# A third quarter buffer, evenly spaced conversions and 128-row stack reads in a fused attention and expert kernel on one core

## The reference, cut to what matters

```python
x = x + tanh(g_xattn) * attention(layernorm(x), ctx)      # x, ctx: 8 x 256 x 512, fp32
x = x + tanh(g_ffn) * experts(layernorm(x))               # 2048 tokens, 512 wide

def attention(x, c, Wq, bq, Wk, bk, Wv, bv, Wo, bo):      # over 256 channels, 16 heads of 16
    q, k, v = Wq @ x + bq, Wk @ c + bk, Wv @ c + bv       # per batch item, 256 x 512
    scores = einsum('bhkt,bhks->bhts', q, k) * 16 ** -0.5
    return Wo @ einsum('bhts,bhks->bhkt', softmax(scores), v) + bo

def experts(x):                                           # 12 experts, the 2 best for a token
    for e in range(12):
        h = silu(x @ w1[e].T) * (x @ w3[e].T)             # 320 hidden columns
        out += (h @ w2[e].T) * weight_of(e)               # softmax of the gate's 2 largest
```

## Time and profile before

| | us |
|---|---|
| median of 3 runs | 824.47 |
| the profiled execution, its span | 824.88, 823.1 |
| PE busy (x4217) | 646.0 |
| DVE busy (x757) | 415.7 |
| ACT busy (x391) | 316.8 |
| POOL busy (x186) | 243.8 |
| mean granted clock of PE | 0.888 |

### The profile page before, as it was taken

One profiled execution on the slowest core, in us unless ns is written; L12 is line 12 of the kernel. 1 busy time (PEld: TensorE's weight loads), 2 busy tenths in 40 slices (PEclk: granted clock), 3 DMA queues, 4 the chain that ended last, 5 costly groups with the idle time before them and its releaser, 6 DMA issues.

```text
span 823.1 us, 13989 instructions
## 1 busy us (share of the span) xinstructions
PE 646.0 (78%) x4217; PEld 282.8 (34%) x4218; DVE 415.7 (50%) x757; ACT 316.8 (38%) x391; POOL 243.8 (30%) x186
## 2 busy tenths in 40 slices
PE   4478897887885977978878654259999999999993
PEld 1112122212221222221221121236666666666661
DVE  5526476566584683774654843563333333333330
ACT  0047655554663554654646510002222222222221
POOL 5223123132240340331210202043344443354422
PEclk9999999889897997997987955559999999999997
DMA  6548669569579587695797636543677787754432
GB/s 205 129 104 204 209 212 293 146 191 310 156 217 293 146 227 262 192 251 159 238 251 211 203 106 230 174 156 63 174 188 195 213 242 201 204 105 92 85 51 39
DMA packets 66405, 150.82 MB, mean 183 GB/s; under 512 B 9973, under 2 KB 15606, under 8 KB 64822
## 3 DMA queue, kind: packets, MB, share of 16 engines
q1 hardware_dynamic: 34576, 72.37, 31.5%
q10 hardware_dynamic: 22150, 55.35, 20.3%
q0 software_dynamic: 9632, 22.55, 14.1%
HBM read 87.85 MB, written 57.93 MB: 177 GB/s over the span
## 4 chain that ended last, share of the span: by engine, by line
PE 50%; DVE 16%; DMA 15%; issue 7%; ACTq 3%; ACT 2%; SPq 2%; POOL 2%; PEldq 1%; POOLq 0%; DVEq 0%
PE S L1365 15%; PE O L1386 8%; DMA wf<-wall 8%; PE O L1229 7%; PE MA L1264 7%; DVE wp L814 4%; PE S L1190 4%; DVE wp L812 4%; DMA out<-yo,slot_out 3%; ACT prob L716 2%; PE S L1352 2%; PE MA L1246 2%; PE MC L1264 2%; ACTq L697 1%; ACTq L691 1%
## 5 line engine op out<-in xcount | busy, mean ns | idle before, releaser
L716 ACT ACTIVATE prob<-S 128x1024 f32<-128x1024 f32 x256 | 244.9, 1025 | 223.5 <-PE S L1190 121.3
L1229 PE MATMUL O<-prob,V 128*32 128x512 f32 x1024 | 154.5, 680 | 0.0
L1365 PE MATMUL S<-W,xT 128*128 x1032 | 150.1, 303 | 1.2 <-issue 1.2
L1190 PE MATMUL S<-Q,K 48*128 48x512 f16 x512 | 93.8, 421 | 69.3 <-ACT prob L716 60.1
L1365 PEld LDWEIGHTS S<-W,xT 128*128 128x128 f16 x1032 | 100.4, 99 | 38.9 <-issue 1.4
L648 POOL DMA_INDIRECT out<-yo,slot_out x43 | 68.2, 1587 | 118.3 <-ACT yo L761 65.4
L1190 PEld LDWEIGHTS S<-Q,K 48*128 48x128 f16 x512 | 19.7, 95 | 209.5 <-ACT prob L716 176.5
L1386 PE MATMUL O<-W,hT 128*128 (+1 forms) x344 | 90.3, 381 | 0.9 <-DVE hT L1161 0.9
L1149 DVE SCALAR_TENSOR_TENSOR hh<-S,act 128x320 f32<-128x320 f32 x43 | 21.1, 492 | 126.9 <-PE S L1365 126.9
L814 DVE SCALAR_TENSOR_TENSOR wp<-wf,wp 128x1024 f16<-128x1024 f32 x48 | 71.4, 1488 | 1.7
L812 DVE TENSOR_SCALAR wp<-wf 128x1024 f16<-128x1024 f32 x48 | 47.0, 979 | 41.9 <-DMA wf<-wall 41.9
(11 more groups left out here) (145 smaller groups left out, 651.5 us busy)
## 6 DMA issues: line engine op xcount, KB each, us to landing
wf<-wall ACTq DMA_DIRECT2D x48, 512.0 KB, 7.6
weight_parts<-wp ACTq DMA_DIRECT2D x48, 512.0 KB, 6.1
W<-weight_parts SPq DMA_DIRECT2D x10, 2048.0 KB, 10.0
k_parts<-ks SPq DMA_DIRECT2D x24, 256.0 KB
q_parts<-qs SPq DMA_DIRECT2D x24, 256.0 KB
K<-k_parts SPq DMA_DIRECT2D x16, 384.0 KB, 7.3
Q<-q_parts SPq DMA_DIRECT2D x16, 384.0 KB, 10.6
ctx<-ctx_in SPq DMA_DIRECT2D x8, 512.0 KB, 10.0
```

Source lines behind the costliest of these rows:

```text
L716: act.activation(prob[:, u % RING, :], S[u % 2][:, :], ACT.Exp, scale=SCALE).then_inc(g.exp, 1)
L1190: last = pe.matmul(S[u % 2][:, s * T:(s + 1) * T], K[par][r0:r0 + rows_, 2 * g4 + n, st * P:(st + 1) * P], Q[par][r0:r0 + rows_, 2 * g4 + ...
L1229: last = pe.matmul(O[g4 % 2][2 * DK * j:2 * DK * (j + 1), :], V[par][:, st, head(g4, j), :], prob[:, u % RING, (j % 2) * T:(j % 2 + 1) * T ...
L1365: last = pe.matmul(ps, xT[par][:, xp * TT + k, :], W[:, bass.ds(off + (w * WCOL + (2 * k + n) * F), F)], start=(k == 0 and (xp, w) == (0, 0)),
```

## The change

1. `wf` has three buffers (`WFS`). Quarters are counted through, 0 to 47, and the load of quarter n+3 is issued behind the store of quarter n. The splits stand in steps (4, 7, 10, 13) in slot 1 and (0, 2, 5, 8, 10, 13) in slots 2 to 7; slot 8 is as before.
2. The context has one buffer for two: its load for item t+1 waits for the low half of item t.
3. The DRAM copies of K and Q have a fourth row group, written once at the start from `wp` with constants (it takes the place of the memsets of the second run). A stack is then read in one transfer of 128 rows.
4. SP's order: K's three writes, Q's two high writes, the read of K, Q's low write, the read of Q. K and Q have semaphores of their own.
5. In slot 0 the low halves of the context, x, K and Q are made by DVE (`low`), not by POOL.
6. The copies into `ocz` are issued in another order. Products on PE are the same.

```diff
+    WFS = 3
-    q_dram = nc.dram_tensor("q_parts", [P // DK, PARTS, DK, CT * T], F16).ap()
+    q_dram = nc.dram_tensor("q_parts", [P // DK, PARTS + 1, DK, CT * T], F16).ap()
-        wf = [sb(f"wf{i}", [P, WQ], F32) for i in range(2)]
+        wf = [sb(f"wf{i}", [P, WQ], F32) for i in range(WFS)]
-        ctx_sb = [sb(f"ctx{i}", [P, CT, T], F32, att) for i in range(2)]
+        ctx_sb = sb("ctx", [P, CT, T], F32, att)
-        KQ_WRITES, KQ_READS = 16 * 2 * PARTS, 16 * 4
+        KQ_WRITES, KQ_READS = 16 * PARTS, 16 * 2
             if t.i is None and t.add == 1:
-                steps, parts = (4, 7, 11, 13), [(At(None, 0, 0), c) for c in range(4)]
+                steps, first = (4, 7, 10, 13), At(None, 0, 0)
...
             else:
-                steps = (2, 4, 7, 11, 12, 13)
...
+                steps = (0, 2, 5, 8, 10, 13)
+                first = At(t.i, 12, 4 + 6 * (t.add - 2)) if t.i is not None else At(None, 0, 4 + 6 * (t.add - 2))
+            return [(v, first.before(-n)) for n, v in enumerate(steps)]
...
-                        wait(sp, g.cl, nxt, 1, -1)
-                        load_ctx(nxt, 1 - par)
+                        wait(sp, g.cl, nxt, 1)
+                        load_ctx(nxt)
...
-                        for half in range(2):
-                            for j in range(GH):
-                                if (half, j) == (1, 0):
+                        for j in (0, 2, 1, 3):
+                            for half in range(2):
+                                if (j, half) == (1, 0):
...
+                        def read(stack, dram):
+                            sp.dma_start(stack[par][:, :, :].rearrange("p (g m) t -> p g (m t)", m=CT),
+                                         dram.rearrange("(g s) r c n -> (s r c) g n", s=2)).then_inc(g.qk, 16)
...
+                        wait(sp, g.kh, t, 1, 1)
+                        write(k_dram, ks, 0, (0, 1), g.kst)
+                        wait(sp, g.kl, t, 1, 1)
+                        write(k_dram, ks, 1, (2,), g.kst)
+                        wait(sp, g.qh, t, 1, 1, s_bog)
+                        write(q_dram, qs, 0, (0, 2), g.qst)
+
+                        wait(sp, g.kst, t, KQ_WRITES, KQ_WRITES, s_bog)
...
+                        read(K, k_dram)
+                        wait(sp, g.ql, t, 1, 1, s_bog)
+                        write(q_dram, qs, 1, (1,), g.qst)
+                        wait(sp, g.qst, t, KQ_WRITES, KQ_WRITES, s_bog)
+                        read(Q, q_dram)
...
+            for n, value in enumerate((SHIFT, 0.0)):
+                pool.memset(wp[n][:, 0, :], value).then_inc(s_padset, 1)
...
+            def store_quarter(q):
+
+                c = q.add % 4
+                wait(act, s_wlo, q, 1, 1, s_bias)
+                act.dma_start(w_dram[bass.ds(over(q, 4).value(), 1), :, :, c * WQ:(c + 1) * WQ]
+                              .rearrange("e p h n -> p (e h) n"), wp[q.add % 2][:, :, :]).then_inc(s_wst[q.add % 2], 16)
+                if q.i is not None or q.add + WFS < QUARTERS:
+                    load_quarter(q.before(-WFS))
...
+            def low(b, parts, f, hi, lo):
+
+                wait(dve, hi, b, 1, 1)
+                dve.tensor_tensor(parts[:, 1], f[:, :, :], parts[:, 0], ALU.subtract).then_inc(lo, 1)
```

More of the change, by code:

```diff
@@ L374, in flamingo_kernel @@
         s_wr = sem("s_wr")
-        s_wf = [sem(f"s_wf{i}") for i in range(2)]
+        s_wf = [sem(f"s_wf{i}") for i in range(WFS)]
         s_whi, s_wlo = sem("s_whi"), sem("s_wlo")
@@ L476, in slot @@
                         wait(sp, g.zst, bc, 16, 16)
-                        for half in range(2):
-                            for j in range(GH):
+                        for j in range(GH):
+                            for half in range(2):
                                 dst0 = 64 * half + DK * j
@@ L494, in slot, with write @@
-                        wait(sp, g.qkst, t, KQ_WRITES, KQ_WRITES, s_bog)
-                        wait(sp, g.full, t, 2 * VS, -2 * VS)
-                        for stack, dram in ((K, k_dram), (Q, q_dram)):
-                            for s in range(2):
-                                sp.dma_start(stack[par][64 * s:64 * s + PARTS * DK, :, :]
-                                             .rearrange("p (g m) t -> p g (m t)", m=CT),
-                                             dram.rearrange("(g s) r c n -> s (r c) g n", s=2)[s]).then_inc(g.qk, 16)
+                        def write(dram, parts, part, rows_, st):
+                            for r in rows_:
+                                sp.dma_start(dram[:, r], parts[:, part].rearrange("p m t -> p (m t)")).then_inc(st, 16)
@@ L584, in slot @@
                     nxt, bc = t.before(-1), t.before(2)
-                    if a:
+                    if t.i is None and t.add == 0:
+                        if not guard:
+                            constants()
+                    elif a:
                         lo_part(t, ks, kf, g.kh, g.kl)
@@ L989, in inverse_sums @@
                     best(g.best, 0, NT - CT)
-                if guard:
-                    for i in range(2):
-                        for r0 in (64 * s + 32 for s in range(2)):
-                            dve.memset(K[i][r0:r0 + 32, :, :], SHIFT).then_inc(s_rows, 1)
-                ctx_high(At(None, 0, 0), 0)
+                first = At(None, 0, 0)
+                ctx_high(first)
                 if not guard:
@@ L998, in attention @@
                     split_projections((0,))
-                x_spread(At(None, 0, 0))
+                low(first, cs, ctx_sb, g.ch, g.cl)
+                x_spread(first)
                 if not guard:
@@ L1002, in attention @@
                     split_projections((1,))
-                x_normed(At(None, 0, 0))
+                x_normed(first)
+                low(first, xs, xn, g.xh, g.xl)
                 slots(dve, slot)
```

125 lines of the change are left out of this document (52 added, 73 removed).

## The result

Twenty executions of each kernel, on one chip: 828.11 us after (823.12 to 835.61) and 824.60 before (816.60 to 833.82). The ratio is 1.0052 with a 95% interval of 1.0029 to 1.0075. The forecast was 780 us. The change made the kernel slower by half a per cent. In every ratio here executions more than 1.5% above the fastest of the same kernel are left out; the medians in us are of all executions.

What follows compares the result with a forecast made beforehand. No engine was full; waits in DVE's list order, chiefly for weight-quarter loads, made the slot's length. Terms -30 - 5 - 3 - 2 - 4 = -44 from 824.9 gave 781, median 780 us; own range 764 to 795, with neighbouring cases 752 to 803.

Steps and rivals of the forecast that it cites:

- The sum a slot: Slots 2 to 6: -7.5 - 1.2 + 2.7 = -6.0 us each, 57.0 to 51.0, so -30 for five.
- The wait taken away, -7.5 a slot: Slots 2 to 6: DVE's wait for weight loads goes, 6.2 us, and with it the slow k0, 1.3 us.
- The copy of v1 waits for the broadcasts, which are no earlier, so I keep the 1.35 us: Step 5: v1's copy leaves the split's shadow but waits for the broadcasts, so PE still waits 1.35 us.
- `zl`, the first link: Ahead of k1's copy: the reciprocal waits for row `zl`, landing in 5.5 us, making the copy 1.9 us late.
- The same three places, 4.0 us a slot, about what the pair cost before: Splits of steps 5, 8, 10 beside POOL: TENSOR_SCALAR 2.03 us instead of 0.69, 4.0 a slot, about the earlier cost.
- The other case that I gave there: Contended splits: if DVE and POOL both ran slowed throughout, 3.1 us more per split, 2 us a slot less gain.
- Other stretches at half clock, -1.2.: Slots 2 to 6: other PE products at half clock, such as value products, partly speed up, 1.2 us a slot.
- Slot 1 and slots 7 and 8, -3, -5 and -2: Slot 1: -3 us (0 to -5); slot 7: -5 (0 to -9); slot 8: -2 (+1 to -6).
- Slot 0, -4: Slot 0: DVE's low halves and the shorter read of Q together give -4 us (+1 to -7).
- Swapped waits: Rival: DVE's list order sets the slot; contended splits and ACT's stores hold PE; 2.5 us a slot, 803 us, chance 0.16.
- slower: Rival: Q's stack comes late behind K's read on SP, PE idles at step 15; 830 us, chance 0.05.
- nothing gained: Rival: the wait only moves to the store of the quarter two before; 823 us, chance 0.04.

Runs made afterwards that it cites:

- run 4: Changed kernel with step 5's product taking xn instead of waiting for the inverse sums, broadcasts still issued (output not the reference's): 794.25 us, 0.9607 of the kernel before.
- run 8: Changed kernel with the inverse sums broadcast by 4 transfers of 64 rows instead of 8 of 16 rows: 849.62 us, 1.0374 of the kernel before.
- run 12: Kernel before the change with step 5's product taking xn instead of the inverse sums, broadcasts still issued (output not the reference's): ratio 0.9891.
- Run 13: Changed kernel with splits in steps (0, 4, 7, 9, 12, 14) in slots 2 to 7, (4, 7, 11, 13) in slot 1: 797.74 us, ratio 0.9664.
- Run 14: Changed kernel with each quarter's store, and the load behind it, three steps behind the split instead of two (two in step 13): 792.65 us, ratio 0.9626.
- run 11: Changed kernel with steps (2, 4, 7, 9, 12, 14) in slots 2 to 7 and slot 0's low halves on POOL: 792.94 us, ratio 0.9630.
- run 17: Changed kernel, its own steps, with stores three steps behind the split, the product behind v1's copy and slot 0's low halves on POOL: 788.35 us, ratio 0.9585.
- run 18: Changed kernel, steps (2, 4, 7, 9, 12, 14), stores three steps behind the split, product behind v1's copy, slot 0's low halves on POOL: 797.83 us, 0.9701.
- run 7: Changed kernel with splits in steps (2, 4, 7, 9, 12, 14) in slots 2 to 7 and (4, 7, 11, 13) in slot 1: 796.97 us, ratio 0.9700.

## Why the prediction was wrong

**Right.** The wait for `wf<-wall` is gone and k0 runs in 1.47 us. Stack reads land in 7.1 us (K) and 6.6 (Q); before, each of the two reads of K took 7.3 and each of Q's 10.6. In slots 1 to 7 nobody waits for them. No split waits for a store. In slot 0 Q's read takes 5.45 us where I took 6. Context in one buffer costs nothing that shows.

**The sum a slot.** It was -7.5 and -1.2 for the wait and the clock, +2.7 for what comes late next: -6.0. Measured is -0.3: -3.35 and -1.03 in the two stretches where the wait had been, +4.06 in the four between. So 3.1 us of the miss lie in the first term, and 2.6 in the other two.

**The wait taken away, -7.5 a slot: mis-sized.** DVE's 6 us and PE's idle time ahead of k0 are gone, but a slot got only 4.4 us shorter there. PE had been working through most of DVE's wait: DVE stood from 252.57 to 260.36, and PE's value products ran until 258.2 (257.11 and 1.06).

**"The copy of v1 waits for the broadcasts, which are no earlier, so I keep the 1.35 us": the first step that failed.** PE's wait is 3.60 us now. I priced `zl`, the first link, at 1.9 us (it showed no wait of that size: 3.4 us in 2 waits in all), and left the rest of the same chain at its old value. But the chain is counted from `osum`: 18.6 us to the product (211.85 to 230.45). In the kernel before, PE's pause between `osum` and k0, the one that I removed, ran beside it, and the split of step 4 filled what was left, so that the product ran without a wait, 21.6 us after `osum` (205.14):

```profile
223.86 1.68 DVE L812 TENSOR_SCALAR wp<-wf 128x1024 f16<-128x1024 f32 x1
225.58 1.23 DVE L814 SCALAR_TENSOR_TENSOR wp<-wf,wp 128x1024 f16<-128x1024 f32 x1
226.72 1.22 DVE L888 TENSOR_TENSOR kf<-ocz 128x1024 f32<-128x1024 f32 x1
```

The change took away both covers, and put two quarters' transfers on the DMA engines during it. Runs 4, 8 and 12 show that this wait reaches the end of the kernel. Run 13 shows that a split in step 4 fills the wait, not that filling it makes the front shorter.

**"The same three places, 4.0 us a slot, about what the pair cost before": the second step that failed.** Three contended splits take 3.72, 3.73 and 3.72 us for 1.92, 5.4 a slot more. The size was a little off. (The other case that I gave there, both instructions slowed throughout, would cost three times 3.1 us, 5.4 more than the 4.0 and not 2.) What I left out is what is queued behind them on another engine: the store on ACT, two steps later, and the exponentials behind it. I had read just this event in the profile before and took it to go with the load. Run 14 takes it away: PE's wait for exponentials falls from 54.2 to 14.4 us, the time by 37. I also took PE's wait for t1 to stay at 3.10 us; it is 4.17 us with the stores as they were and 4.53 with later ones.

**"Other stretches at half clock, -1.2."** They moved to v2 and to t0 to the logits, 8.71 to 10.83 us.

**Slot 1 and slots 7 and 8, -3, -5 and -2.** Slot 1 lasts 1.3 us longer. From k0 of slot 7 to the logits of slot 8 it is 103.6 us for 99.6; with later stores it is 93.3. Later stores shorten these slots too, by 4.8 and 10.3 us; which cause does how much there I haven't separated.

**Slot 0, -4.** The first scores are 0.55 us later. I counted DVE's low halves against Q's chain alone. They stand ahead of the copy of k0 as well: k1 starts at 18.59 for 15.50. And Q's low write took 8.91 us behind K's read, which eats most of what the shorter read gives (4.48 and 10.73 before, 8.91 and 5.45 after). With POOL making them (run 11) the first scores come at 43.96.

**The rivals.** "Swapped waits", 803 us at 0.16, named the mechanism: contended splits, and ACT's stores holding the exponentials (in two of the three places). Its 2.5 us a slot of remaining gain was too kind; it was 0.3. The measured 828 us lie nearer to "slower", 830, and "nothing gained", 823, but by luck: PE waits for Q only in slot 0 (6.4 us), and no split waits for a store. The two causes that I had as separate small terms, or not at all, overlap: 27 us or so come back without the one (run 4 less its control), 37 with later stores (run 14), and 38 with both treated (run 17). Most of what I forecast was there to be had: 788 us with the change's own steps and three small edits. What is left in it is PE's wait for DVE's copy of t0 behind the split of step 10, 4.5 us a slot.

## What to carry to other kernels

Before a wait is removed, list what ran in its shadow, and follow each such chain from its fixed start to its last user; a link that waited for nothing before may have been hidden by the very pause that goes. For every instruction that gets slower or moves, ask what stands behind its signal in the in-order list of another engine; moving a DMA issue one step later may be worth more than the buffer (37 us here, the buffer 11 at its best). When one wait falls, look at whether another has taken its place in the same gap before the gain is counted. And when steps move, look at which transfers travel together: in run 18 the stacks' writes and reads became the bound.

## What the runs showed of the hardware

- Small transfers are slowed by large ones of the other queue: 32 KB of inverse sums land in 1.5 us (median, runs 7 and 14) and in 3.6 to 3.7 where a quarter's store and load are issued within a microsecond of them (the changed kernel, run 13).
- A broadcast of the same bytes in 4 transfers of 64 rows was 4 us slower to land than in 8 of 16 rows, though issued 1.8 us faster. Each wide one had 5 updates of its semaphore, each narrow one 16 (run 8 and the changed kernel). The stacks' writes, whose outermost dimension in DRAM is 8, have 9 each (216 for 24).
- Products behind three idle stretches ran at half speed: k0 in 2.74 us for 1.47 after 6.83 us idle (before), v2 in 1.46 for 0.83 after 3.60, t1 in 1.11 for 0.66 after 4.17. After 1.90 us idle the scores at 249.15 ran at full speed, 0.39 us for two.
- A split beside POOL's subtraction takes 1.8 us more in each of the three places, either in its first instruction (2.50 us for 0.69) or in its second (3.04 for 1.23), and not in both, as the one pair before did, where two of POOL's instructions followed each other. The lock for a whole instruction, as the Trainium skill has it (SBUF — State Buffer, "SBUF: two separate sides"), agrees with that.
